# Graph kernel: dense adjacency built two pairs to a bank and emptied by two engines, one-hots by scalar comparison, type embeddings in one matmul, packed slices

## The chip, the cores and the metric

The kernel runs on one core of a Trainium2 chip. Times are device microseconds of one execution; three runs of the kernel before gave 7442.04, 7473.25 and 7475.92 us, a median of 7473.25.

## The reference

Two message-passing layers with residual and layer norm over a graph of 6250 nodes and 206,250 edges sorted by destination. The first is a two-layer mean aggregation. The second, which the change is about, has three relational convolutions with 5 edge types; the first of them takes a node's 128 features joined with the 128 of its type's embedding (3 types):

```python
def rgcn_conv(x, src, dst, etype, W, root, bias):
    seg = dst * R + etype                      # R = 5 relations
    agg = segment_sum(x[src], seg, n * R)
    cnt = segment_sum(ones, seg, n * R)
    agg = where(cnt > 0, agg / max(cnt, 1), 0).reshape(n, R, -1)
    return einsum('nrd,rdk->nk', agg, W) + x @ root + bias

h = concatenate([x, node_emb[node_type]], -1)
h = relu(rgcn_conv(h, ..., W1, root1, b1))     # 256 -> 256
h = relu(rgcn_conv(h, ..., W2, root2, b2))     # 256 -> 128
h = relu(rgcn_conv(h, ..., W3, root3, b3))     # 128 -> 128
```

## The kernel before, in words

The first 1480 us or so make the mean-aggregation layer, and as a by-product, codes of the edges. Then conv 1, 2 and 3 run (v = 0, 1, 2 in the code), each as its own loop over half ticks, written out on every engine; what stands in a half tick on an engine is run in that order, and semaphores join the engines.

**Groups.** A tick (two half ticks) handles one group of 4 tiles of 128 edges. GpSimd gathers the messages of the source nodes by four indirect DMAs (L1373), up to 6 groups ahead. VectorE makes a one-hot of where each edge's sum goes (L1628, 4 groups ahead), TensorE multiplies (12 matmuls at L1386, and in conv 1 four narrow ones at L1390 for the types), and VectorE adds the result to running sums (L1650, L1651). Conv 1 has 403 groups and covers all nodes so; conv 2 and 3 have 235 each, for 28 of 49 tiles of nodes.

**Windows.** Every 16 ticks or so the sums of 256 nodes are whole. In `finish`, VectorE scales them (L1690, for features and types), clears them (L1697) and makes node_hot, the one-hot of the nodes' types (L1726). TensorE then makes the products with W1 in fp32 (L1461 to L1464, both halves of the 256 outputs): per half and relation one with the features and one with the types, and the two of the root. After ScalarE's relu TensorE makes the rows of the next convolution's table (L1470, L1444), which ScalarE and VectorE split in three bf16 pieces (VectorE's part at L1707 and L1712, where it waits for ScalarE), and SP stores them.

**The dense adjacency.** For the last 21 tiles of nodes conv 2 and 3 use a dense matrix of edge counts in place of gathers. It is built within conv 1, beside the groups. In a tick VectorE makes the one-hots of 4 pairs of nodes (`dense_onehots`, L1637, two buffers), TensorE builds 4 pairs, one matmul of 490 columns each, into two banks by turns (`build`, L1401), and ScalarE copies each bank to `stage` as fp8 (`evict`, L1523): a pair's two columns go next to each other, at a step of 32 bytes. Every 16 pairs ScalarE issues three DMAs that store the stage (L1532). 336 ticks, from the third of conv 1 on, have such one-hots. In conv 2 and 3 SP loads the matrix in slices (L1246, three for a chunk and relation) and the table's rows in pieces, and TensorE multiplies (L1421), some 22 matmuls in a tick.

## Time and profile before

| | |
|---|---|
| runs | 7442.04, 7473.25, 7475.92 us |
| profiled execution, own time | 7472.03 us |
| its span | 7469.8 us |
| TensorE (PE) busy | 5533.5 us, 74% |
| weight loads (PEld) | 3186.3 us |
| VectorE (DVE) busy | 2387.7 us, 32% |
| ScalarE (ACT) busy | 2078.3 us, 28% |
| GpSimd (POOL) busy | 3856.8 us, 52% |
| mean granted clock of TensorE | 0.793 |

Busy time is from start to end of an instruction's work; instructions of one engine that overlap are counted once. The clock is a share of full speed. In a timeline, rows of an engine that follow each other with the same line and shape are merged, with their count behind an x, and the idle time before them stands in brackets with what ended it. A releaser "issue" is nothing that the profile shows, "remote" is one that it can't name. A matmul in fp32 leaves two records.

### The profile page before, as it was taken

What the parts mean: (1) busy time and instruction counts of PE and PEld (TensorE: products, weight loads), DVE (VectorE), ACT (ScalarE), POOL (GpSimd) and SP (SyncE); (2) the same over time, 40 slices, a digit from 0 to 9 for tenths busy, and PEclk for the clock granted to TensorE, in tenths of its full rate; (3) what the DMA queues carried; (4) which work ended last, traced back from release to release, by engine and by line L of the source; (5) the groups of instructions that cost most, each with busy time, mean ns of one, the idle gap of its engine ahead of it and who ended that gap; (6) DMA issues with size and microseconds to landing.
All of it is one profiled execution on the core that took longest, in us unless ns stands there. A gap on an engine that the chain in (4) does not pass through costs nothing.

```text
span 7469.8 us, 91271 instructions
## 1 busy us (share of the span) xinstructions
PE 5533.5 (74%) x35088; PEld 3186.3 (43%) x35088; DVE 2387.7 (32%) x5451; ACT 2078.3 (28%) x3054; POOL 3856.8 (52%) x3575
## 2 busy tenths in 40 slices
PE   2777799956677666777667546888888878888887
PEld 1454466523333333333333233444444544454444
DVE  6776641233333333433333211111111211111112
ACT  2444430046565655666555000000000000000000
POOL 4000000076666666767665553666666656666665
PEclk6888899956666666666666566999999989999999
DMA  2222226433333333333333223455455444444443
GB/s 72 118 85 101 97 103 239 185 98 109 91 103 95 109 87 98 102 101 98 101 95 101 67 83 110 140 168 167 137 169 163 140 150 142 145 143 137 138 143 108
DMA packets 689816, 903.43 MB, mean 121 GB/s; under 512 B 73166, under 2 KB 605444, under 8 KB 685412
## 3 DMA queue, kind: packets, MB, share of 16 engines
q1 hardware_dynamic: 335292, 453.57, 18.0%
q0 software_dynamic: 169216, 348.44, 16.8%
q10 hardware_dynamic: 184872, 95.53, 4.4%
q8 instruction: 282, 4.62, 0.2%
q14 instruction: 154, 1.26, 0.1%
HBM read 692.22 MB, written 205.05 MB: 120 GB/s over the span
## 4 chain that ended last, share of the span: by engine, by line
PE 44%; ACT 12%; issue 9%; another core or an unknown queue 8%; DVE 4%; ACTq 2%; DVEq 0%; DMA 0%; POOL 0%; POOLq 0%
PE bank L1421 21%; ACT stage L1523 12%; PE bank L1386 7%; PE bank L1461 4%; PE bank L1462 4%; PE bank L1401 3%; PE bank L1444 2%; ACTq L1532 2%; PE bank L1390 1%; DVE scaled L1690 1%; PE bank L1463 1%; PE bank L1464 1%; DVE type_scaled L1690 1%; PE bank L1470 1%
## 5 line engine op out<-in xcount | busy, mean ns | idle before, releaser
L1373 POOL DMA_INDIRECT messages<-table,src_rows x2552 | 2873.0, 1126 | 1582.2 <-issue 711.9
L1421 PE MATMUL bank<-slices,pieces 128*128 128x384 fp8e4 x10290 | 1983.5, 337 | 363.8 <-issue 351.1
L1523 ACT CAST stage<-bank 128x490 fp8e4<-128x490 f32 x1344 | 1458.5, 1270 | 1063.8 <-PE bank L1401 820.0
L1421 PEld LDWEIGHTS bank<-slices,pieces 128*128 128x128 bf16 x10290 | 988.5, 100 | 1206.1 <-issue 702.3
L1373 POOL DMA_INDIRECT messages<-table,rel_rows x940 | 900.0, 957 | 586.1 <-issue 251.4
L1401 PE MATMUL bank<-rel_hot,lo_dense_hot 128*128 128x490 bf16 x1344 | 647.2, 521 | 675.3 <-ACT stage L1523 506.7
L1386 PE MATMUL bank<-group_hot,messages 128*128 128x120 bf16 x10476 | 875.6, 245 | 238.4 <-issue 99.8
L1651 DVE TENSOR_TENSOR sums<-sums,bank 128x120 f32 x873 | 236.5, 271 | 2299.9 <-remote 1823.0
L1386 PEld LDWEIGHTS bank<-group_hot,messages 128*128 128x128 bf16 x10476 | 777.0, 113 | 395.5 <-issue 239.3
L1650 DVE TENSOR_TENSOR type_sums<-type_sums,bank 3x120 f32 x403 | 107.9, 268 | 1913.2 <-PE bank L1390 1280.6
L1355 POOL IOTA iota_rel_i<- 128x490 int32 x1 | 1.4, 1395 | 1355.8 <-DMA table<-typed_rows 1355.8
L1401 PEld LDWEIGHTS bank<-rel_hot,lo_dense_hot 128*128 128x128 bf16 x1344 | 120.4, 103 | 1107.7 <-ACT stage L1523 787.7
L966 ACT CAST adjacency<-bank 128x400 bf16<-128x400 f32 x784 | 391.9, 504 | 436.3 <-PE bank L844 431.7
L868 PE MATMUL bank<-adjacency,x_pieces 128*128 128x384 bf16 (+1 forms) x2499 | 485.6, 337 | 0.0
L844 PE MATMUL bank<-q_hot,lo_hot 128*128 128x100 bf16 x3136 | 232.1, 222 | 264.2 <-DVE rd_hot L1048 255.5
L1461 PE MATMUL bank<-scaled,w 128*128 128x256 f32 (+1 forms) x500 | 300.5, 705 | 149.2 <-issue 149.2
L1598 ACT ACTIVATE rstd<-moments,eps 128x2 f32<-128x2 f32 (+1 forms) x21 | 6.2, 296 | 1440.6 <-DVE moments L1779 1068.6
L868 PE MATMUL bank<-adjacency,h_pieces 128*128 128x384 bf16 (+1 forms) x2499 | 398.9, 320 | 0.0
L1637 DVE TENSOR_TENSOR rel_hot<-iota_rel,rel_dense 128x1960 bf16<-128x1960 f16 x336 | 389.8, 1160 | 0.0
L1578 ACT ACTIVATE h_wide<-h_wide 128x256 f32<-128x256 f32 (+1 forms) x21 | 9.5, 452 | 1231.0 <-issue 633.1
L1628 DVE TENSOR_TENSOR group_hot<-iota,group_code 128x480 bf16<-128x480 f16 x873 | 347.6, 399 | 1.6
L844 PEld LDWEIGHTS bank<-q_hot,lo_hot 128*128 128x128 bf16 x3136 | 194.2, 106 | 340.2 <-DVE rd_hot L1048 253.1
(249 smaller groups left out, 4344.6 us busy)
## 6 DMA issues: line engine op xcount, KB each, us to landing
slices<-relations_d SPq DMA_DIRECT2D x140, 768.0 KB
adjacency_d<-adjacency SPq DMA_DIRECT2D x15, 4704.0 KB, 14.5
adjacency<-adjacency_d SPq DMA_DIRECT2D x15, 4704.0 KB, 15.0
slices<-relations_d SPq DMA_DIRECT2D x70, 816.0 KB
relations_d<-stage ACTq DMA_DIRECT2D x168, 320.0 KB
messages<-table,src_rows POOLq DMA_INDIRECT x2552
inverse<-inverse_d SPq DMA_DIRECT2D x52, 640.0 KB
relations_d<-stage ACTq DMA_DIRECT2D x84, 340.0 KB
```

The lines of the kernel that those rows point to most:

```text
L844: mm = pe.matmul(to[:, m * PAIR_COLS:(m + 1) * PAIR_COLS], lo_hot[:, i % 2, pair, :], q_hot[:, i % 2, pair, :], start=True, stop=True)
L868: mm = pe.matmul(bank[SUM_BANKS[k % 2]][:, 0:cols], pieces[:, h, piece, :], adjacency[HALF[c]][:, h, 0:cols], start=(m == 0), stop=(m == N ...
L966: act.copy(to, pairs).then_inc(evicted, 1)
L1373: pool.indirect_dma_start(messages[:, i % MESSAGES, t, 0:ROWS[v]], None, GATHERED[v], bass.IndirectOffsetOnAxis(ap=rows[:, e:e + 1], axis= ...
L1386: mm = pe.matmul(to[:, 0:GROUP_COLS], messages[:, i % MESSAGES, t, piece * P:(piece + 1) * P], group_hot[:, i % MESSAGES, t, :], start=(t ...
L1401: pe.matmul(bank[REL_BANKS[p % 2]][:, 0:REL_COLS], lo_dense_hot[:, b % 2, m, :], rel_hot[:, b % 2, m, :], start=True, stop=True).then_inc( ...
L1421: mm = pe.matmul(bank[DENSE_BANKS[K % 2]][:, 0:CHUNK], pieces[M % PIECE_RING][:, tile % PIECE_TILES, piece * P:(piece + 1) * P], slices[:, ...
L1461: pe.matmul(to, w1[:, r, f_cols], scaled[:, r, 0:cols], start=(r == 0), stop=False)
L1462: pe.matmul(to, emb_1[:, r * WIDE + half * P:r * WIDE + (half + 1) * P], type_scaled[:, r, 0:cols], start=False, stop=False)
L1523: act.copy(stage[:, u % 2, :, 2 * m:2 * m + 2], bank[REL_BANKS[p % 2]][:, 0:REL_COLS].rearrange("p (c d) -> p c d", d=2), saturate=False). ...
L1628: vec.tensor_tensor(group_hot[:, i % MESSAGES, :, :].rearrange("p k (c t) -> p k c t", t=2), iota16[:, 0:GROUP_COLS].rearrange("p (c t) -> ...
L1637: op = vec.tensor_tensor(hot[:, b % 2, :, :].rearrange("p u (c t) -> p u c t", t=2), iota[:, 0:cols].rearrange("p (c t) -> p c t", t=2).un ...
```

## The change

1. *Builds.* Two pairs (a couple) are built at once, in two parts: part 0 has the columns of tiles 0 to 24 (250 a pair), part 1 those of tiles 25 to 48 (240 a pair). Each part has one bank of its own, that holds both pairs. ScalarE copies part 0 out, VectorE part 1, each pair's two bytes next to the other's, so four in a row. Each part has its own semaphore. The stage's store (two DMAs, ScalarE's queue) comes 3 half ticks after its last couple.
2. *One-hots of the builds.* In place of two comparisons of two tensors for 4 pairs there are eight of a tensor with one fp32 number per partition, two for each pair.
3. *Type embeddings.* The 5 products of types and the root's of a half become one, whose 18 rows are the 6 x 3 types; SP copies the scaled type sums and node_hot of each window to partitions 32 to 49 by six DMAs, and the embeddings once. TensorE waits for them behind the sixth product of the first half, and no longer for node_hot.
4. *Slices.* Two for a chunk and relation (25 and 24 tiles) instead of three, loaded without gaps; 3 of them in the ring instead of 4, and 8 pieces of the table instead of 9.

```diff
-SLICE_TILES = (17, 16, 16)
+SLICE_TILES = (25, 24)
-SLICE_RING = 4
+SLICE_RING = 3
-PIECE_RING = PIECE_BLOCKS + 2
+PIECE_RING = PIECE_BLOCKS + 1
...
+            sp.wait_ge(emb_kept, 1)
+            for r in range(RELATIONS + 1):
+                at = EMB_AT + r * NODE_TYPES
+                sp.dma_start(emb_1[at:at + NODE_TYPES, 0:WIDE], emb_1[0:NODE_TYPES, r * WIDE:(r + 1) * WIDE] if r < RELATIONS else emb_root[:, :]).then_inc(emb_in, 16)
             for w in range(WINDOWS_1):
                 first = w * WINDOW
+                sp.wait_ge(scaled_made, w + 1)
+                sp.wait_ge(nodes_spread, w + 1)
+                sp.wait_ge(window_psum, w)
+                for r in range(RELATIONS + 1):
+                    at, cols = EMB_AT + r * NODE_TYPES, window_cols(0, w)
+                    sp.dma_start(type_scaled[at:at + NODE_TYPES, 0, 0:cols], type_scaled[0:NODE_TYPES, r, 0:cols] if r < RELATIONS else node_hot[:, 0:cols]).then_inc(typed_in, 16)
...
-            def build(p):
-
-                b, m = divmod(p, BATCH)
+            def build(j):
+
+                b, m = divmod(2 * j, BATCH)
                 if m == 0:
                     pe.wait_ge(rel_hot_made, b + 1)
-                if p >= 2:
-                    pe.wait_ge(rel_evicted, p - 1)
-                pe.matmul(bank[REL_BANKS[p % 2]][:, 0:REL_COLS], lo_dense_hot[:, b % 2, m, :], rel_hot[:, b % 2, m, :], start=True, stop=True).then_inc(rel_psum, 1)
+                for n in range(SLICES):
+                    if j:
+                        pe.wait_ge(rel_evicted[n], j)
+                    of_part = slice(2 * SLICE_FIRST[n], 2 * (SLICE_FIRST[n] + SLICE_TILES[n]))
+                    width = 2 * SLICE_TILES[n] * RELATIONS
+                    for q in range(2):
+                        hot = rel_hot[:, b % 2, m + q, :].rearrange("p (r c) -> p r c", r=RELATIONS)[:, :, of_part]
+                        mm = pe.matmul(bank[REL_BANKS[n]][:, q * width:(q + 1) * width], lo_dense_hot[:, b % 2, m + q, :], hot, start=True, stop=True)
+                    mm.then_inc(rel_psum, 1)
...
-                        pe.wait_ge(nodes_spread, w + 1)
...
+                            if half:
+
+                                pe.wait_ge(typed_in, 16 * (RELATIONS + 1) * (w + 1))
+                                pe.matmul(to[0], emb_all[:, f_cols[0]], typed_all[:, 0:cols], start=False, stop=True)
                             for r in range(RELATIONS):
-                                pe.matmul(to, w1[:, r, f_cols], scaled[:, r, 0:cols], start=(r == 0), stop=False)
-                                pe.matmul(to, emb_1[:, r * WIDE + half * P:r * WIDE + (half + 1) * P], type_scaled[:, r, 0:cols], start=False, stop=False)
-                            pe.matmul(to, w1_root[:, f_cols], x1_T[:, nodes], start=False, stop=False)
-                            mm = pe.matmul(to, emb_root[:, f_cols], node_hot[:, 0:cols], start=False, stop=True)
-                        mm.then_inc(window_psum, 1)
+                                pe.matmul(to[half], w1[:, r, f_cols[half]], scaled[:, r, 0:cols], start=(r == 0), stop=False)
+                            pe.matmul(to[half], w1_root[:, f_cols[half]], x1_T[:, nodes], start=False, stop=False)
+                        pe.matmul(to[1], emb_all[:, f_cols[1]], typed_all[:, 0:cols], start=False, stop=True).then_inc(window_psum, 1)
...
+        def evict(engine, n, j):
+
+            u, m = divmod(j, STAGE_COUPLES)
+            engine.wait_ge(rel_psum, j * SLICES + n + 1)
...
+            from_bank = bank[REL_BANKS[n]][:, 0:4 * SLICE_TILES[n] * RELATIONS].rearrange("p (q c d) -> p c q d", q=2, d=2)
+            to = stage[:, u % 2, rows, 4 * m:4 * m + 4].rearrange("p c (q d) -> p c q d", q=2)
+            if n == 0:
+                engine.copy(to, from_bank, saturate=False).then_inc(rel_evicted[n], 1)
+            else:
+                engine.tensor_copy(to, from_bank, saturate=False).then_inc(rel_evicted[n], 1)
...
                 if b >= 2:
-                    vec.wait_ge(rel_psum, (b - 1) * BATCH)
-                for hot, codes, iota, cols in ((lo_dense_hot, lo_dense, iota16, P), (rel_hot, rel_dense, iota_rel, REL_COLS)):
-                    op = vec.tensor_tensor(hot[:, b % 2, :, :].rearrange("p u (c t) -> p u c t", t=2),
-                                           iota[:, 0:cols].rearrange("p (c t) -> p c t", t=2).unsqueeze(1).broadcast_to([P, BATCH, cols // 2, 2]),
-                                           codes[:, pairs, :].unsqueeze(2).broadcast_to([P, BATCH, cols // 2, 2]), ALU.is_equal)
+                    vec.wait_ge(rel_psum, (b - 1) * SLICES * BATCH // 2)
+                for m in range(BATCH):
+
+                    vec.tensor_scalar(lo_dense_hot[:, b % 2, m, :], iota16[:, :], lo_dense[:, b * BATCH + m:b * BATCH + m + 1], None, ALU.is_equal)
+                    op = vec.tensor_scalar(rel_hot[:, b % 2, m, :], iota_rel[:, :], rel_dense[:, b * BATCH + m:b * BATCH + m + 1], None, ALU.is_equal)
                 op.then_inc(rel_hot_made, 1)
...
+                    if v == 0 and 0 <= couple_at(half - 1) < COUPLES:
+                        evict(vec, 1, couple_at(half - 1))
```

VectorE, at the end of a window within conv 1, before the change (group_hot is the groups' one-hot, sums and type_sums the running sums, scaled and type_scaled the finished window):

```order
L1628 TENSOR_TENSOR group_hot<-iota_49,group_code 128x480 [waits group_psum]
L1644 TENSOR_LOAD base_i
L1650 ISA [waits sums_added,group_psum]
L1650 TENSOR_TENSOR type_sums<-type_sums,bank 3x120
L1651 REGISTER_ALU
L1651 TENSOR_TENSOR sums<-sums,bank 128x120
L1637 TENSOR_TENSOR lo_dense_hot<-iota_49,lo_dense 128x512 [waits rel_psum]
L1637 TENSOR_TENSOR rel_hot<-iota_rel,rel_dense 128x1960
L1690 TENSOR_TENSOR scaled<-sums,inverse 128x1280 [waits window_psum,inverse_in1,sums_added]
```

The same place on VectorE, with the change:

```order
L1690 ISA [waits sums_added,group_psum]
L1690 TENSOR_TENSOR type_sums<-type_sums,bank 3x120
L1691 REGISTER_ALU
L1691 TENSOR_TENSOR sums<-sums,bank 128x120
L1678 TENSOR_SCALAR lo_dense_hot<-iota_49,lo_dense 128x128 [waits rel_psum]
L1679 TENSOR_SCALAR rel_hot<-iota_rel,rel_dense 128x490
L1678 TENSOR_SCALAR lo_dense_hot<-iota_49,lo_dense 128x128
L1679 TENSOR_SCALAR rel_hot<-iota_rel,rel_dense 128x490
L1678 TENSOR_SCALAR lo_dense_hot<-iota_49,lo_dense 128x128
L1679 TENSOR_SCALAR rel_hot<-iota_rel,rel_dense 128x490
L1678 TENSOR_SCALAR lo_dense_hot<-iota_49,lo_dense 128x128
L1679 TENSOR_SCALAR rel_hot<-iota_rel,rel_dense 128x490
L1560 CAST stage<-bank 128x120x4 [waits rel_psum] x2
```

Two copies of part 1 (one at the end of each half tick) now stand between the one-hots and what followed them; both wait for a build. The first belongs to the couple that was built ahead of the group whose sums were just added.

TensorE in a tick of builds, before the change (group_hot and messages are the group's, rel_hot and lo_dense_hot the builds'):

```order
L1401 MATMUL bank<-rel_hot,lo_dense_hot 128x490 [waits rel_evicted] x3
L1386 MATMUL bank<-group_hot,messages 128x120 [waits gathered0,group_hot_made,sums_added]
L1386 MATMUL bank<-group_hot,messages 128x120 x11
L1390 MATMUL bank<-group_hot,messages 3x120 x4
L1401 MATMUL bank<-rel_hot,lo_dense_hot 128x490 [waits rel_evicted,rel_hot_made]
```

TensorE with the change, with the block of a window in fp32 (L1495, L1496; L1493 and L1497 are the type products) in front of the second couple of a tick, and the group behind it (L1408, L1412):

```order
L1495 MATMUL bank<-scaled,w_126 128x256 [waits wide_made,scaled_made]
L1495 MATMUL bank<-scaled,w_126 128x256 x4
L1496 MATMUL bank<-x_T,w_root 128x256
L1493 MATMUL bank<-type_scaled,emb_130 128x256 [waits typed_in]
L1428 MATMUL bank<-rel_hot,lo_dense_hot 128x250 [waits rel_evicted0]
L1428 MATMUL bank<-rel_hot,lo_dense_hot 128x250
L1428 MATMUL bank<-rel_hot,lo_dense_hot 128x240 [waits rel_evicted1]
L1428 MATMUL bank<-rel_hot,lo_dense_hot 128x240
L1408 MATMUL bank<-group_hot,messages 128x120 [waits gathered3,group_hot_made,sums_added]
L1408 MATMUL bank<-group_hot,messages 128x120 x11
L1412 MATMUL bank<-group_hot,messages 3x120 x4
L1428 MATMUL bank<-rel_hot,lo_dense_hot 128x250 [waits rel_evicted0,rel_hot_made]
```

Where a build waited for a copy two builds back, each part now waits for the copy of the same part one couple back.

## Rows read from the trace of the kernel before

**Rows 1.** Busy time by stretch: us, busy by engine, granted clock, DMA share, GB/s
```profile
1521.00:4076.00 2555.00, 1801.79 (x8034) 890.35 (x8034) 953.34 (x1929) 1503.07 (x1512) 1694.97 (x1346) 0.63 0.34 98
4140.00:4560.00 420.00, 225.36 (x1129) 133.14 (x1126) 92.76 (x222) 17.06 (x36) 199.36 (x198) 0.59 0.23 66
```

**Rows 2.** The chain of waits in 1521 to 4076 us, by line
```profile
by line: ACT stage L1523 34.1%; PE bank L1461 9.1%; PE bank L1462 9.0%; issue 7.8%; PE bank L1401 7.5%; PE bank L1386 6.3%; ACTq L1532 4.7%; PE bank L1444 4.6%; another core or an unknown queue 4.3%; PE bank L1390 2.7%; PE bank L1463 1.8%; 
```

**Rows 3.** By tile or line: count, ns min/median/max, first and last start
```profile
L1637 DVE TENSOR_TENSOR rel_hot<-iota_rel,rel_dense x336: 1158/1160/1173, 1521.6 to 4075.8; 128x1960 bf16<-128x1960 f16 x168
...
L1461 PE MATMUL bank<-scaled,w x500: 421/634/797, 1641.2 to 4570.4; 128*128 128x256 f32 x160, 128*128 128x128 f32 x7
```

**Rows 4.** Timeline, ticks with builds: start us, us, engine, line, operation
```profile
2989.79 0.79 PE L1386 MATMUL bank<-group_hot,messages 128*128 128x120 bf16 x12
2990.51 0.37 PE L1390 MATMUL bank<-group_hot,messages 128*3 128x120 bf16 x4
...
2996.31 1.40 PE L1386 MATMUL bank<-group_hot,messages 128*128 128x120 bf16 x12
...
3001.06 0.59 PE L1401 MATMUL bank<-rel_hot,lo_dense_hot 128*128 128x490 bf16 x1 [0.44 <-ACT stage L1523]
...
3001.44 1.41 PE L1386 MATMUL bank<-group_hot,messages 128*128 128x120 bf16 x12
...
3002.78 0.56 PE L1390 MATMUL bank<-group_hot,messages 128*3 128x120 bf16 x4
3002.92 0.95 POOL L1373 DMA_INDIRECT messages<-table,src_rows  x1 [0.30 <-issue]
...
3003.47 0.27 DVE L1650 TENSOR_TENSOR type_sums<-type_sums,bank 3x120 f32 x1 [2.93 <-issue]
...
3003.86 0.41 DVE L1637 TENSOR_TENSOR lo_dense_hot<-iota,lo_dense 128x512 bf16<-128x512 f16 x1
3003.89 4.32 ACT L1523 CAST stage<-bank 128x490 fp8e4<-128x490 f32 x4 [0.82 <-PE bank L1401]
3004.18 2.33 POOL L1373 DMA_INDIRECT messages<-table,src_rows  x1 [0.30 <-issue]
3004.19 1.16 DVE L1637 TENSOR_TENSOR rel_hot<-iota_rel,rel_dense 128x1960 bf16<-128x1960 f16 x1
...
3005.28 0.39 DVE L1628 TENSOR_TENSOR group_hot<-iota,group_code 128x480 bf16<-128x480 f16 x1
...
3017.96 1.41 PE L1386 MATMUL bank<-group_hot,messages 128*128 128x120 bf16 x12
```

**Rows 5.** Timeline around the block of one window
```profile
3031.63 2.48 DVE L1690 TENSOR_TENSOR scaled<-sums,inverse 128x1280 f32<-128x1280 f32 x1
...
3032.96 1.41 PE L1386 MATMUL bank<-group_hot,messages 128*128 128x120 bf16 x12
...
3039.29 0.34 DVE L1726 TENSOR_SCALAR node_hot<-types_in,j_col 3x256 f32<-3x256 int32 x1
...
3039.73 1.19 PE L1461 MATMUL bank<-scaled,w 128*128 128x256 f32 x2 [3.95 <-issue]
...
3068.09 1.41 PE L1386 MATMUL bank<-group_hot,messages 128*128 128x120 bf16 x12
```

**Rows 6.** VectorE's groups by shape (count, busy, mean ns), and one stretch of its timeline
```profile
L1088 DVE TENSOR_TENSOR mean<-bank,inv_deg 128x384 f32<-128x384 f32 x32 | 17.8, 556 | 342.9 <-PE bank L868 180.5 <-DMA residual_d<-mean 162.4
L584 DVE TENSOR_SCALAR passed<-j,last_f 128x3136 bf16<-128x3136 f16 x13 | 12.4, 1031 | 0.0
L1088 DVE TENSOR_TENSOR mean<-bank,inv_deg 128x128 f32<-128x128 f32 x2 | 0.6, 292 | 9.8 <-DMA x_rows<-residual_d 5.9 <-PE bank L868 4.0
...
9.09 12.39 DVE L584 TENSOR_SCALAR passed<-j,last_f 128x3136 bf16<-128x3136 f16 x13
```

**Rows 7.** The page's costliest groups: count, busy us, mean ns, idle before
```profile
L1421 PE MATMUL bank<-slices,pieces 128*128 128x384 fp8e4 x10290 | 1983.5, 337 | 363.8 <-issue 351.1
...
L966 ACT CAST adjacency<-bank 128x400 bf16<-128x400 f32 x784 | 391.9, 504 | 436.3 <-PE bank L844 431.7
```

More of the change, by code:

```diff
@@ L476, in keep_span @@
                     turned_codes = bank[CODE_BANKS[n]][:, 0:width // 2].bitcast(f16)
+                    if n == 0 and s >= FIRST_DENSE_SPAN:
+                        first = max(0, FIRST_DENSE_PAIR - s * SPAN)
+                        act.copy(lo_plain[:, SPAN_PAIRS[s]], turned_codes[:, first:width])
                     act.copy(to[:, cols, :], turned_codes.unsqueeze(2).broadcast_to([P, width, 2])).then_inc(span_kept, 1)
@@ L485, in keep_rel @@
                 turned_codes = bank[CODE_BANKS[0]][:, first // 2:(first + width) // 2].bitcast(f16)
[L486 removed]
+                act.copy(rel_code[:, cols], turned_codes).then_inc(rel_kept, 1)
             keep_span(0)
@@ L1506, in conv_tensor @@
                     if v == 0:
-                        first = (half - 2 * (REL_TICK + 1)) * (BATCH // 2)
-                        for p in range(max(0, first), min(first + BATCH // 2, DENSE_PAIRS)):
-                            build(p)
+                        if 0 <= couple_at(half) < COUPLES:
+                            build(couple_at(half))
                     if v == 2 and half - 2 in plan.task_end:
```

91 lines of the change are left out of this document (49 added, 42 removed).

## The prediction

> **What bounds the kernel now.** I read the stretches first, then the chain of waits, then one tick in the timeline. The change touches the first relational convolution, in which ticks with dense builds run from 1521.6 to 4075.8 us: 336 of them, one per pair of one-hot instructions [rows 3], 7.6 us each. In that stretch no engine is full: TensorE is busy 1802 of 2555 us at a granted clock of 0.63, ScalarE 1503, VectorE 953, GpSimd 1695 [rows 1]. The chain says who is waited for: ScalarE's copies out of the banks (stage L1523) are 34% of it, the two families of wide fp32 matmuls L1461 and L1462 9% each [rows 2].
>
> The timeline shows how. Two ScalarE copies stand between the builds and two beside the group's 16 matmuls; four take 4.32 us, 1.07 each [rows 4], and every fourth tick also issues three DMAs on ScalarE. Four ticks from 2996.31 to 3017.96 take 21.65 us, 5.4 each [rows 4]. The end of a window puts in one block of 24 fp32 products: from one group at 3032.96 to the next at 3068.09 are 35.1 us, of which the block from 3039.73 is about 27.6, so 1.15 us a product (the profile has two records for one) [rows 5]. It waited for node_hot, made at 3039.29 + 0.34 [rows 5]. Blocks start from 1641.2 to 4570.4, 500 records at 20 a block, so 25 blocks [rows 3]: about 20 beside the builds (every 122 us until 4075.8), 4 full ones behind them, and a last one of half width. The 316 build ticks without a block share 2554 - 20 x 35.1 = 1852 us.
>
> GpSimd is near but not the bound: a gather takes 0.95 us and 0.30 between two, yet one that starts within VectorE's run of one-hots takes 2.33 [rows 4]. With one such gather a tick that is 4 x 1.25 + 1.38 = 6.4 us a tick at worst; in the stretch it is busy 1695 of 2555 us.
>
> **The change, part by part.** *Where the new wait sits.* A bank now holds two pairs of one part of the columns, so a build needs its own bank emptied, with no second bank to alternate with. Part 0 is emptied by ScalarE, part 1 by VectorE. VectorE's copy for the second couple of a tick stands behind the next group's adds and behind the eight new one-hot instructions, and TensorE's second part of the following build waits for it, in front of everything else on TensorE. So a loop through both engines closes twice a tick. At TensorE's lower clock, from one VectorE copy's end to its like a tick later:
> - TensorE starts after 0.10 (3039.63 to 3039.73 [rows 5]); 480 columns at the pace of 490 in 0.38 (3001.06 to 3001.44); the group from 3001.44 to 3002.78 + 0.56, 1.90; VectorE starts at 3003.47, 0.13 later; its two adds until 3003.86, 0.39 [rows 4]: 2.90.
> - Eight TENSOR_SCALARs. Thirteen of 3136 f16 elements take 12.39 us, the last lasting 1.03, so 0.947 from start to start [rows 6]. On VectorE a column from PSUM costs (556 - 292) / 256 = 1.03 ns [rows 6]; at a quarter of that 3136 cost 0.81, and 0.14 stay per instruction. So 490 columns 0.27, 128 columns 0.17, and four of each 1.7 us, against 3003.86 to 3005.28 = 1.42 for the two instructions of now [rows 4].
> - VectorE's copy, 480 columns of fp32 from PSUM: 292 ns at 128 columns plus 352 x 1.03 = 0.65.
> - Release 0.10, the part's 480 columns with their latency 0.52, release 0.13, the second copy 0.65: 1.40.
>
> Together 6.65 us. At the high clock (a group from 2989.79 to 2990.51 + 0.37 is 1.09 instead of 1.90, and 0.2 less on each part) it is 5.45. The granted 0.63 of [rows 1] is 26% of the time at 2.4 GHz and the rest at 1.2, so 6.34 on average. ScalarE, with two copies and fewer DMAs a tick, falls off the path; what it did cost ends, and the tick of 5.4 becomes 6.34. The runs of stores and the ticks with table matmuls gain and lose a little each; I take +1.0 us for each of 316 ticks: **+316**.
>
> The copy's price is not in the trace: ScalarE's of the same kind costs 1.07 for 490, while its fp32-to-bf16 copy of 400 takes 0.50 [rows 7]. From below it is 0.57 (0.07 fixed, as between the two one-hots that start at 3003.86 and 3004.19, 512 columns in 0.33 at 0.26 + 0.07), from above ScalarE's 1.06. I take 0.65, the rows of VectorE itself.
>
> The Trainium skill (SBUF — State Buffer, under "Door 1: The DMA port swizzle") says that two accesses in one 16-byte line suffice for full rate. The copy of now writes two bytes at a step of 32 and takes 1.07 us, so this trace does not agree; by the rule the new copy with four bytes in a row would be 0.65, and if ScalarE's rate holds per element, 1.06.
>
> *The type embeddings.* Twelve of the 24 products are of type embeddings; two take their place, so 14 stay: 10 x 1.15 = 11.5 us less. Beside builds the gain is smaller: VectorE goes through scale, memsets and node_hot from 3031.63 to 3039.56 (7.9 us) [rows 5], and only then through 0.33 group one-hots, 0.39 adds, 1.7 and 0.65 to the copy that TensorE needs in front of the block. So from the group's start the block begins after 10.6 + 0.5 instead of 6.8, takes 16.1, and two builds follow: 28.0 instead of 35.1, or **-144** for 20. Behind the builds this doesn't hold; there the block also need not wait for node_hot (3.2 us), but its seventh product waits for six small copies by DMA, issued one after the other on SP behind node_hot (I take 1.7 us of a possible -3 to +5): -13 for each of 4, -7 for the last: **-59**.
>
> *Row pieces.* VectorE's four subtractions per window now stand in the loop; half of each is hidden by the part's matmuls: **+12** for 20 windows.
>
> *Packed slices, ring of 3, ring of pieces 8.* The loads become one run a partition. TensorE waited for nothing named there: 1.98 ms of dense matmuls with 351 us of "issue" before them [rows 7]. I cost it at nothing; it is bounded by those 351 us on one side and, if the shorter ring of pieces is late at four changes of relation, by 4 x 10 us on the other. Earlier stages: a few copies of 0.6 us, nothing.
>
> Sum on the profiled execution, 7472.0 us (median of the three 7473.25): +316 - 144 - 59 + 12 = +125, so **7597 us**.
>
> The Trainium skill (VectorE: DVE Perf Modes, "Rules for kernel authors") advises few VectorE instructions rather than fused ones, since each pays a fixed cost. [rows 6] agree with 0.14 us each; it speaks against eight one-hots in place of two, which the fourfold rate (same page, "The perf-mode tier table") would otherwise favour. By element rate alone they would take 0.6 us, by the rule 1.7.
>
> **Rivals.** *VectorE's pieces are cheap (faster).* If only 0.07 is fixed per instruction, one-hots take 1.2 and a copy 0.57, the loop 5.99 and 5.68 on average: +0.34 x 316 + 12 - 156 (each block starts 0.6 sooner) - 59 = -96, 7376 us. For it: the spacing of the two one-hots of now. Against: two kinds of rows with 0.14 or more [rows 6]. It decides from a loop of 5.9 us down, where the block's gain wins.
> *The fp8 copy costs on VectorE what it costs on ScalarE.* 1.06 instead of 0.65 twice: +0.82 x 316 + 8, 7864 us. For it: the same destination, steps of 32 bytes. Against: twice as many bytes in a row, another engine.
> *The clock.* If TensorE is granted 2.4 GHz half of the time, the loop is 6.05 and the sum +32, 7505 us. Behind the builds, with TensorE busy 225 of 420 us, it was 0.59 [rows 1], so a looser load doesn't promise it.
> *The slices.* If a third of the 351 us came from their many small packets: 7480 us. Nothing in the rows ties them.
> *ScalarE's relief shows and no loop forms.* It would need VectorE's copy in front of its one-hots; the order shows it behind.
>
> **How the numbers follow.** Forecast 0.50 (7520 to 7690); dear copy 0.16; cheap pieces 0.17; clock 0.09 and slices 0.08, mostly within 0.5%, which is 7436 to 7511 and about what a measurement tells from no change. So faster 0.20, same 0.12, slower 0.68. The range of 7430 to 7870 leaves out the cheap end and what lies above the dear copy.
>
> **What would show it.** In the profile after: groups of four ticks 25 us apart instead of 21.65; TensorE's second part released by VectorE and not ScalarE; ScalarE busy under half of the stretch; eight TENSOR_SCALARs in 1.7 us; a VectorE copy of 0.65; blocks of 16 us and 28 from group to group; later convolutions of equal length. I am wrong if the first part's release by ScalarE still ends the waits, if the tick stays under 5.9 us, or if the gain lies behind 4600 us.

## The result, and the profile after

The changed kernel takes 7379.94 us (median of 4 runs, 7372.54 to 7387.85) against 7461.24 of the kernel before (4 runs): ratio 0.9883, 95% interval 0.9862 to 0.9904. That is 1.2% faster, where 7597 us and 1.7% slower were forecast; it lies 50 us below the lower end of the range. Its profiled execution took 7384.1 us, span 7382.3.

Of the 87.5 us between the two spans, this is where they come and go. A "tick" is the time from one group to the next; there are 336 with builds, 20 of them with a block of fp32 products in them. The builds are counted from VectorE's first one-hots to its last.

| us | before | after | difference | forecast |
|---|---|---|---|---|
| start of the builds | 1521.6 | 1531.8 | +10 | 0 |
| 316 build ticks without a block | 1852 (5.86 each) | 2122 (6.715 each) | +270 | +328 |
| 20 ticks over a block | 702 (35.1 each) | 401 (20.05 each) | -301 | -144 |
| last one-hots to the last block | 494.6 | 427.3 | -67 | -59 |
| last block to the end | 2899.4 | 2900.2 | +1 | 0 |

(+328 is +316 and the +12 for the row pieces.) The stretch with builds and the one behind them, columns as in [rows 1]:

```profile
1532.00:4055.00 2523.00, 1450.11 (x8970) 918.27 (x8970) 1442.00 (x4609) 455.12 (x845) 1439.71 (x1342) 0.64 0.35 99
4140.00:4470.00 330.00, 149.13 (x1012) 109.24 (x1011) 80.89 (x208) 17.07 (x36) 181.00 (x184) 0.65 0.29 82
```

ScalarE's busy time fell from 1503 to 455 us, VectorE's rose from 953 to 1442, and TensorE's is 352 us less at nearly the same mean clock. The chain of waits in 1532 to 4055 us, which answers to [rows 2]:

```profile
by line: PE bank L1428 14.6%; PE bank L1408 13.2%; DVE rel_hot L1679 13.1%; DVE stage L1560 12.2%; DVE lo_dense_hot L1678 8.7%; issue 7.2%; PE bank L1412 5.7%; PE bank L1495 5.1%; PE bank L1473 4.9%; DVE sums L1691 3.4%; DVE scaled L1730 1.
```

ScalarE's copy, 34% before, is gone from it, and VectorE's one-hots (L1678, L1679) and copy (L1560) are 34% together. The products of a block are 5.1% on the new line L1495, where L1461 and L1462 had 18. First and last start by tile and line, as in [rows 3]:

```profile
L1679 DVE TENSOR_SCALAR rel_hot<-iota_rel,rel_dense x1344: 330/332/522, 1531.8 to 4054.8; 128x490 bf16<-128x490 f16 x192
...
L1495 PE MATMUL bank<-scaled,w x500: 379/622/796, 1661.9 to 4482.1; 128*128 128x256 f32 x160, 128*128 128x128 f32 x7
```

One plain tick in the timeline, at the place of [rows 4]:

```profile
3000.45 1.41 PE L1408 MATMUL bank<-group_hot,messages 128*128 128x120 bf16 x12
3001.78 0.56 PE L1412 MATMUL bank<-group_hot,messages 128*3 128x120 bf16 x4
...
3002.68 0.26 DVE L1691 TENSOR_TENSOR sums<-sums,bank 128x120 f32 x1
3002.87 0.23 DVE L1678 TENSOR_SCALAR lo_dense_hot<-iota,lo_dense 128x128 bf16<-128x128 f16 x1
...
3004.55 0.64 DVE L1560 CAST stage<-bank 128x480 fp8e4<-128x480 f32 x1
3005.24 0.53 PEld L1428 LDWEIGHTS bank<-rel_hot,lo_dense_hot 128*128 128x128 bf16 x4 [2.84 <-DVE stage L1560]
...
3005.86 0.66 DVE L1560 CAST stage<-bank 128x480 fp8e4<-128x480 f32 x1 [0.68 <-PE bank L1428]
...
3006.95 1.41 PE L1408 MATMUL bank<-group_hot,messages 128*128 128x120 bf16 x12
```

The circle, the loop of waits through TensorE and VectorE, stands as the prediction drew it: group, adds, eight one-hots in 1.68 us (3002.87 to 3004.55), copy 0.65, second part of the next build, copy 0.65, group. It takes 6.50 us at the lower clock (6.65 forecast). The block, at the place of [rows 5]:

```profile
3037.01 4.48 PE L1495 MATMUL bank<-scaled,w 128*128 128x256 f32 x10
...
3041.29 1.06 PE L1496 MATMUL bank<-x_T,w_root 128*128 128x256 f32 x2
...
3042.28 0.87 PE L1493 MATMUL bank<-type_scaled,emb 18*128 18x256 f32 x2
3043.08 2.43 PE L1495 MATMUL bank<-scaled,w 128*128 128x256 f32 x10
...
3045.34 0.59 PE L1496 MATMUL bank<-x_T,w_root 128*128 128x256 f32 x2
...
3046.49 0.60 PE L1428 MATMUL bank<-rel_hot,lo_dense_hot 128*128 128x250 bf16 x4
```

It is over in 9.5 us (3037.01 to 3046.49), not in 16.1; the 20 blocks beside builds last 8.9 in the mean, 8.2 to 9.6. Its first five wide products take 4.28 us, 0.86 each, and the five of the second half 2.26, 0.45 each. The clock of the same time (us, TensorE busy, granted clock as a share of 2.4 GHz, DMA share, GB/s):

```profile
3037.00:3040.00 3.00, 3.00 (x9) 0.50 0.17 41
3040.00:3043.00 3.00, 3.00 (x8) 0.55 0.00 0
3043.00:3046.50 3.50, 3.50 (x16) 1.00 0.00 0
3046.50:3058.00 11.50, 6.94 (x59) 1.00 0.43 128
```

and of the block before the change, 48 records without a gap:

```profile
3040.00:3067.00 27.00, 27.00 (x48) 0.50 0.16 42
```

So both halves of the block's gain have to be explained: what it costs per product, and that TensorE comes up to 2.4 GHz in it and stays there for a while behind it.

### The profile page after: what moved, and what is told of

Same layout as the page of the kernel before. It is cut to its first block, busy times and chain, and to the rows that moved or that the text cites. A ratio compares the mean times of both kernels' runs of the same rounds, so it can differ in the third digit from the quotient of the medians.

```text
span 7382.3 us, 95103 instructions
## 1 busy us (share of the span) xinstructions
PE 5100.1 (69%) x35932; PEld 3189.8 (43%) x35932; DVE 2881.2 (39%) x8139; ACT 1023.3 (14%) x2385; POOL 3605.2 (49%) x3575
## 4 chain that ended last, share of the span: by engine, by line
PE 44%; DVE 18%; issue 8%; another core or an unknown queue 7%; DVEq 1%; DMA 1%; SPq 0%; ACT 0%; POOL 0%; POOLq 0%
PE bank L1450 22%; PE bank L1408 9%; PE bank L1428 5%; DVE rel_hot L1679 4%; DVE stage L1560 4%; DVE lo_dense_hot L1678 3%; PE bank L1412 2%; PE bank L1495 2%; PE bank L1473 2%; DVE sums L1691 1%; DVE scaled L1730 1%; DVE type_scaled L1730 1%; DVE sums L1737 1%; PE bank L1521 0%
## 5 line engine op out<-in xcount | busy, mean ns | idle before, releaser
L1395 POOL DMA_INDIRECT messages<-table,src_rows x2552 | 2621.1, 1027 | 1773.1 <-PE bank L1412 802.7
L1428 PE MATMUL bank<-rel_hot,lo_dense_hot 128*128 128x240 bf16 (+1 forms) x2688 | 651.6, 362 | 1093.3 <-DVE stage L1560 1013.5
L1408 PE MATMUL bank<-group_hot,messages 128*128 128x120 bf16 x10476 | 911.3, 252 | 251.3 <-issue 132.9
L1408 PEld LDWEIGHTS bank<-group_hot,messages 128*128 128x128 bf16 x10476 | 817.7, 118 | 379.4 <-issue 227.4
L1428 PEld LDWEIGHTS bank<-rel_hot,lo_dense_hot 128*128 128x128 bf16 x2688 | 213.7, 111 | 1449.2 <-DVE stage L1560 1227.9
L1558 ACT CAST stage<-bank 128x500 fp8e4<-128x500 f32 x672 | 387.1, 576 | 2117.6 <-PE bank L1428 1992.0
L1560 DVE CAST stage<-bank 128x480 fp8e4<-128x480 f32 x672 | 434.1, 646 | 184.6 <-PE bank L1428 182.2
L1679 DVE TENSOR_SCALAR rel_hot<-iota_rel,rel_dense 128x490 bf16<-128x490 f16 x1344 | 450.5, 335 | 0.0
L1678 DVE TENSOR_SCALAR lo_dense_hot<-iota,lo_dense 128x128 bf16<-128x128 f16 x1344 | 336.3, 250 | 0.3
L877 PEld LDWEIGHTS bank<-adjacency,h_pieces 128*128 128x128 bf16 x2499 | 238.4, 98 | 151.8 <-issue 3.8
```

Of the source, the lines that this page charges most:

```text
L877: mm = pe.matmul(bank[SUM_BANKS[k % 2]][:, 0:cols], pieces[:, h, piece, :], adjacency[HALF[c]][:, h, 0:cols], start=(m == 0), stop=(m == N ...
L1395: pool.indirect_dma_start(messages[:, i % MESSAGES, t, 0:ROWS[v]], None, GATHERED[v], bass.IndirectOffsetOnAxis(ap=rows[:, e:e + 1], axis= ...
L1408: mm = pe.matmul(to[:, 0:GROUP_COLS], messages[:, i % MESSAGES, t, piece * P:(piece + 1) * P], group_hot[:, i % MESSAGES, t, :], start=(t ...
L1428: mm = pe.matmul(bank[REL_BANKS[n]][:, q * width:(q + 1) * width], lo_dense_hot[:, b % 2, m + q, :], hot, start=True, stop=True)
L1558: engine.copy(to, from_bank, saturate=False).then_inc(rel_evicted[n], 1)
L1560: engine.tensor_copy(to, from_bank, saturate=False).then_inc(rel_evicted[n], 1)
```

## Experiments

Theory A: the products of 3 rows, in turn with those of 128, are what keeps TensorE at 1.2 GHz in the block, and each costs more than its columns. Rival B: the looser loop ahead of the block lets the clock rise. Rival C: the gain is the number of products.

Runs of one letter ran on one chip, each letter on a chip of its own. On that of the f runs the kernel before took 7462 us, as in the result; on the other three 6853 to 6857. Each ratio is against the kernel before on the same chip. The table puts their profiles side by side (builds here from TensorE's first to its last; "block" is the mean of 20 from group to group over a block, "tick" what is left of the builds for each of the other 316; "to last block" and "to end" follow one another).

| kernel | us | ratio [95%] | block | tick | builds | to last block | to end |
|---|---|---|---|---|---|---|---|
| c0 before | 6860 | | 35.3 | 5.71 | 2512 | 387 | 2456 |
| c1 changed | 6840 | 0.997 [0.996, 0.998] | 20.0 | 6.74 | 2531 | 347 | 2454 |
| e1 changed, old block | 7298 | 1.065 [1.063, 1.067] | 39.7 | 6.82 | 2949 | 386 | 2456 |
| e2 before, new block | 6497 | 0.948 [0.947, 0.950] | 18.7 | 5.76 | 2192 | 347 | 2450 |
| e3 narrow ones grouped | 6589 | 0.961 [0.960, 0.963] | 22.9 | 5.70 | 2260 | 355 | 2453 |
| e4 24 of 128 rows | 6509 | 0.949 [0.948, 0.951] | 19.3 | 5.73 | 2198 | 350 | 2454 |
| d1 24 of 3 rows | 6702 | 0.977 [0.975, 0.978] | 28.7 | 5.73 | 2384 | 361 | 2458 |
| d2 64 and 128 in turn | 6855 | 0.999 [0.999, 1.000] | 35.5 | 5.70 | 2510 | 385 | 2455 |
| f1 24 of 64 rows | 7296 | 0.977 [0.974, 0.979] | 28.5 | 5.84 | 2417 | 452 | 2896 |
| f2 64 rows grouped | 7110 | 0.951 [0.948, 0.954] | 19.9 | 5.96 | 2282 | 411 | 2893 |
| d3 packed slices alone | 6806 | 0.992 [0.991, 0.994] | 35.5 | 5.54 | 2461 | 387 | 2460 |
| c2 copy first | 6288 | 0.918 [0.916, 0.919] | 18.0 | 5.13 | 1980 | 348 | 2456 |
| c3 both copies by ScalarE | 6226 | 0.909 [0.907, 0.910] | 19.5 | 4.83 | 1916 | 359 | 2449 |
| d4 c3, type rows sooner | 6217 | 0.907 [0.905, 0.908] | 14.0 | 5.12 | 1897 | 359 | 2456 |

**e1, the changed kernel with the old block.**

```diff
...
-                        pe.matmul(to[1], emb_all[:, f_cols[1]], typed_all[:, 0:cols], start=False, stop=True).then_inc(window_psum, 1)
...
+                            for r in range(RELATIONS):
+                                pe.matmul(to, w1[:, r, f_cols], scaled[:, r, 0:cols], start=(r == 0), stop=False)
+                                pe.matmul(to, emb_1[:, r * WIDE + half * P:r * WIDE + (half + 1) * P], type_scaled[:, r, 0:cols], start=False, stop=False)
...
```

> The changed kernel with the type embeddings of the first convolution put back as they were: 24 products a block, every second one of 3 rows, no copies by SyncE. Theory A (the 3-row products keep TensorE's granted clock at 0.50): the block goes back to about 27 us and from group to group over it 35 us, so 20 blocks x 15 us and the 67 us behind the builds come back: 7380 + 301 + 67 = about 7748 us. Rival B (TensorE idles longer ahead of a block in the new loop, and that, not the products, let the clock rise): the block shows a clock above 0.7 with the 24 products too and takes about 20 us, 7600 us or less.

The block is back at 39.7 us, and inside it TensorE is busy without a gap at a clock of 0.50:

```profile
2362.00:2390.00 28.00, 28.00 (x55) 0.50 0.00 1
```

Rival B falls: the new loop does not raise the clock by itself. The time of 7748 us was not met because this chip is faster elsewhere; against the changed kernel (c1, on another chip of the same pace) it is +458 us, where +368 was expected: the old block costs 4.3 us more from group to group in the new loop than in the old, though it lasts as long by itself (27.5 and 27.6 us).

**e2, the kernel before with the new block alone.** The twelve narrow products become two of 18 rows, with SyncE's copies of the rows; nothing else changes.

```diff
...
-                                pe.matmul(to, emb_1[:, r * WIDE + half * P:r * WIDE + (half + 1) * P], type_scaled[:, r, 0:cols], start=False, stop=False)
...
+                        pe.matmul(to[1], emb_all[:, f_cols[1]], typed_all[:, 0:cols], start=False, stop=True).then_inc(window_psum, 1)
```

> The kernel before with only the type embeddings changed (one product of 18 rows a half in place of six of 3, the rows gathered by SyncE). Theory A (narrow products hold the clock): the block takes about 9.5 us here as well, 20 x -15 us in the loop and -60 behind it: 7461 - 301 - 60 = 7100 us. Rival B (the lighter loop of the changed kernel gave the clock back): the 14 products stay at a clock of 0.50 and 16 us, 20 x -7 - 59 = 7460 - 200 = 7260 us. Rival C (the gain came from the builds): 7400 us or more.

356 us come off: 20 x 16.6 in the blocks and 40 behind the builds, less 16 in the other ticks. But the block itself is not the 9.5 us of Theory A. It lasts 15.0 in the mean, because TensorE waits 3.4 to 5.8 us behind the sixth product for SyncE's copies; in each of the 20 blocks the clock falls back to 0.50 in this wait or within 2 us behind it:

```profile
2370.00 0.59 PE L1481 MATMUL bank<-x_T,w_root 128*128 128x256 f32 x2
2376.26 1.22 PE L1478 MATMUL bank<-type_scaled,emb 18*128 18x256 f32 x2 [5.67 <-DMA type_scaled<-node_hot]
```

In the changed kernel the block starts later in the tick, when the copies are there, and has no such wait beside builds. So this one part of the change, with its wait, is worth 5.2%; all of it together is worth 0.3% on such a chip (c1), so the rest of the change costs nearly what this part earns.

**e3, the same 24 products in another order.**

```diff
                             for r in range(RELATIONS):
                                 pe.matmul(to, w1[:, r, f_cols], scaled[:, r, 0:cols], start=(r == 0), stop=False)
-                                pe.matmul(to, emb_1[:, r * WIDE + half * P:r * WIDE + (half + 1) * P], type_scaled[:, r, 0:cols], start=False, stop=False)
                             pe.matmul(to, w1_root[:, f_cols], x1_T[:, nodes], start=False, stop=False)
+                            for r in range(RELATIONS):
+                                pe.matmul(to, emb_1[:, r * WIDE + half * P:r * WIDE + (half + 1) * P], type_scaled[:, r, 0:cols], start=False, stop=False)
```

> The kernel before with the same 24 products a block in another order: in each half the six of 128 rows first, then the six of 3 rows. Theory A1 (a narrow product costs or holds the clock wherever it stands): the first half's wide products start at 1.2 GHz, the narrow ones hold it there, block 24 to 27 us, time 7400 to 7461 us. Theory A2 (the alternation does it: weights of 3 and of 128 rows in turn): block 9.5 us for the wide ones and 3 to 5 us for the narrow ones, about 14 us, -12 x 21 = 7200 us.

Nothing is taken away, and 264 us come off. The clock in one block, by runs of products (128 rows, 3 rows, 128 rows, 3 rows):

```profile
2388.40:2393.80 5.40, 5.33 (x12) 0.50 0.22 59
2393.80:2396.60 2.80, 2.80 (x13) 0.98 0.39 95
2396.60:2401.10 4.50, 4.50 (x13) 0.62 0.28 72
2401.10:2404.00 2.90, 2.90 (x14) 1.00 0.36 93
```

It rises at the end of a run of 128 rows, falls back behind the run of 3 rows, and rises again. The narrow products then run at 0.45 us each. The block lasts 15.3 us in the mean, nearer to A2's 14 than to A1's 24 to 27, and -264 us is near A2's -252.

**e4, 24 products of 128 rows.**

```diff
-                                pe.matmul(to, emb_1[:, r * WIDE + half * P:r * WIDE + (half + 1) * P], type_scaled[:, r, 0:cols], start=False, stop=False)
+                                pe.matmul(to, w1[:, r, f_cols], scaled[:, r, 0:cols], start=False, stop=False)
...
-                            mm = pe.matmul(to, emb_root[:, f_cols], node_hot[:, 0:cols], start=False, stop=True)
+                            mm = pe.matmul(to, w1_root[:, f_cols], x1_T[:, nodes], start=False, stop=True)
```

> The kernel before with 24 products a block, all of 128 rows: each narrow product is replaced by a repeat of the wide one beside it, so the type embeddings are left out and the rest is counted twice. Theory A (width, not number): the clock rises inside the block as in the changed kernel, 5 products x 0.86 + 19 x 0.41 = 12 us against 27.0, -15 x 20 - 60: about 7110 us although no product is taken away. Rival D (the number of products is what the block costs): 24 products stay at 1.15 us each, 7461 us or more.

Rival C (D in the text above) falls: as many products as before, more arithmetic, and the time of e2 within 12 us. (That the two are so near doesn't price the ten products more: e2 has its wait instead. The block lasts 12.6 us here and 8.9 in the changed kernel.) The block at work, and two of its products at the higher clock, 0.43 apart:

```profile
2373.00:2375.70 2.70, 2.70 (x7) 0.50 0.14 39
2375.70:2383.70 8.00, 8.00 (x38) 0.99 0.35 86
...
2376.67 0.59 PE L1461 MATMUL bank<-scaled,w 128*128 128x256 f32 x2
2377.10 0.59 PE L1462 MATMUL bank<-scaled,w 128*128 128x256 f32 x2
```

**c0 and c1, both kernels again on a chip of the faster kind.**

> The kernel before, unchanged, for its profile on the chip of this call. On the chip of the last call it took 6853 us against 7461 beside the changed kernel, and its conv 2 and 3 ended 2450 us after the last block in the three kernels derived from it, against 2900 us. Theory: the difference sits behind the builds, where the trace of the first chip has gaps of TensorE that it puts down to issue (351 us at the dense products), and these gaps are gone here; the block is 35 us or a little more, as in the first trace.

> The changed kernel, unchanged, on the chip of this call. Worked out from the run with the old block there (7298 us, 39.3 us over a block, last block at 4840): 20 x (39.3 - 20.1) = 385 and about 65 behind the builds come off, 6850 us: 1.00 of the kernel before. If the two parts add up in another way (Rival: the copies by SyncE cost more where the rest is faster), 6950 us or more.

Both expectations hold: 2456 us from the last block to the end against 2899, and the group of L1421, with 351 us of "issue" before it in [rows 7], has none:

```profile
L1421 PE MATMUL bank<-slices,pieces 128*128 128x384 fp8e4 x10290 | 1789.6, 330 | 0.0
```

The changed kernel is 0.3% faster here, not 1.2%. In the kernel before ScalarE bounds the loop, and on the chip of the result its copies also waited 146 us for issue and 89 for an unknown queue in 1525 to 3900 us, against 79 and nothing here; the changed kernel's ticks (6.715 and 6.74) are the same on both. Why the chips differ was not tried.

**c2, VectorE's copy at the head of the tick.**

```diff
                 for half in range(plan.end):
+                    if v == 0 and 0 <= couple_at(half - 1) < COUPLES:
+                        evict(vec, 1, couple_at(half - 1))
                     if half % 2 == 0 and half < plan.half_ticks:
```

(and taken out behind the one-hots.)

> The changed kernel with VectorE's copy of the even half put at the head of the tick, ahead of the one-hots and of the addition. Theory (the tick is a circle: addition 0.45, one-hots 1.68, copy 0.65, build, group 1.9): one of the two copies leaves the circle, the plain tick goes from 6.47 to 5.6-5.8 us, 316 x -0.8 = -250 us against the changed kernel. Rival (TensorE's own work at 1.2 GHz sets the tick): 6.3 us or more, -50 at most.

-552 us against c1, twice what was expected. Most of it is the circle. Two groups at 1.2 GHz now start 5.25 us apart, where the changed kernel needs 6.50:

```profile
2754.76 1.40 PE L1408 MATMUL bank<-group_hot,messages 128*128 128x120 bf16 x12
2760.01 1.41 PE L1408 MATMUL bank<-group_hot,messages 128*128 128x120 bf16 x12
```

With the one copy the part of a build and the two releases between the copies leave the circle too, the last 1.40 us of the prediction's list, and 6.65 - 1.40 is 5.25. That is about 316 x 1.25 = 395 us, an estimate; 40 more are in the blocks (18.0 for 20.0). The rest, some 117 us, goes with the clock. The busy time and clock of TensorE in 1600 to 3300 us, of c1 and of c2:

```profile
1600.00:3300.00 1700.00, 982.43 (x6047) 0.64 0.35 100
```

```profile
1600.00:3300.00 1700.00, 1109.68 (x7755) 0.74 0.45 128
```

In the tighter loop TensorE's mean clock is 0.74 instead of 0.64, and a group of twelve matmuls that takes 1.41 us at 1.2 GHz takes 0.79 at 2.4, so the circle gets shorter again. No run separates this share.

**c3, both parts copied by ScalarE.**

```diff
                             evict(act, 0, j)
+                            evict(act, 1, j)
...
-                    if v == 0 and 0 <= couple_at(half - 1) < COUPLES:
-                        evict(vec, 1, couple_at(half - 1))
```

> The changed kernel with both parts of a bank couple copied by ScalarE (0.576 us measured for 500 columns), none by VectorE. Theory (VectorE's order holds the bank): ScalarE needs 4 x 0.6 = 2.4 us of a tick, the banks come free at once, and the tick falls to what four gathers on GpSimd take, 4 x 1.3 = 5.2 us: 316 x -1.25 = -400 us against the changed kernel. Rival (ScalarE's copy becomes the bound again as in the kernel before, 1.07 us each): 4 x 1.1 = 4.4 us and the tick stays at 5.9 or more, -180 us at most.

-614 us against c1, more than expected, and by another way than the tick of 5.2. The copies cost ScalarE no more than VectorE:

```profile
L1558 ACT CAST stage<-bank 128x500 fp8e4<-128x500 f32 x1344 | 699.2, 574 | 1173.1 <-PE bank L1428 1161.9 <-issue 4.7 <-DMA relations_d<-stage 1.4
```

The new bound is GpSimd, which waits only 4 us for another engine. Its busy time in 1600 to 3300 us, and its waits there:

```profile
1600.00:3300.00 1700.00, 1336.23 (x1195) 0.75 0.46 132
```

```profile
POOL messages L1395 <- issue: 360.1, 1182, 0.3
POOL messages L1395 <- PE bank L1412: 4.0, 13, 0.3
```

1336 and 360 make 1696 of 1700 us, 1.42 for each of 1195 gathers. 336 ticks of four are 1908 us, and the builds take 1916.

**d1, 24 products of 3 rows.**

```diff
-                                pe.matmul(to, w1[:, r, f_cols], scaled[:, r, 0:cols], start=(r == 0), stop=False)
+                                pe.matmul(to, emb_1[:, r * WIDE + half * P:r * WIDE + (half + 1) * P], type_scaled[:, r, 0:cols], start=(r == 0), stop=False)
...
```

> The kernel before with 24 products a block of 3 rows each, the wide ones replaced by repeats of the narrow ones (the terms of the neighbours and of the node itself are left out of the first convolution's output). Theory N (products of 3 rows leave the granted clock at 0.50 however long TensorE is busy with them): the block shows 0.50 throughout and takes as long as before, 27 us and 35 us from group to group; 6857 us, ratio 0.99 to 1.00. Rival X (only the turn from 3 rows to 128 and back holds the clock): it rises as with 24 wide ones, block 12 to 15 us, -15 x 20 us: 6510 us, ratio 0.95.

**d2, 64 rows in turn with 128.**

```diff
-                                pe.matmul(to, emb_1[:, r * WIDE + half * P:r * WIDE + (half + 1) * P], type_scaled[:, r, 0:cols], start=False, stop=False)
+                                pe.matmul(to, w1[0:64, r, f_cols], scaled[0:64, r, 0:cols], start=False, stop=False)
...
```

> The kernel before with each narrow product replaced by one of 64 rows (the upper half of the wide one beside it, so the type embeddings are left out and half of the other rows are counted twice). If the height of the short products decides, this lies between the block of 24 wide ones (19.3 us from group to group, 6509 us) and the one of before (35.3 us, 6857 us). Theory N with 64 rows as good as 128: 6510 us; Rival X (any turn between two heights): 6857 us.

Theory N holds for the clock in d1 (0.50 throughout) and not for the time: 153 us come off. In d2 the time of before comes back to 1 us, with none of its narrow products. One block of d1, and one of d2, each with two of its products:

```profile
2205.30:2226.10 20.80, 20.76 (x49) 0.50 0.31 77
...
2206.32 1.06 PE L1462 MATMUL bank<-type_scaled,emb 3*128 3x256 f32 x2
2207.18 1.06 PE L1461 MATMUL bank<-type_scaled,emb 3*128 3x256 f32 x2
```

```profile
2238.80:2266.50 27.70, 27.68 (x49) 0.50 0.22 55
...
2239.94 1.22 PE L1462 MATMUL bank<-scaled,w 64*128 64x256 f32 x2
2241.09 1.22 PE L1461 MATMUL bank<-scaled,w 128*128 128x256 f32 x2
```

(The height of a product is the number of its rows; a turn is the change from one height to another.) At the same clock 24 products take 20.8 us without a turn and 27.7 with one at each: they start 0.853 apart in d1 (the mean) and 1.15 in d2, so a turn costs 0.30 us at 1.2 GHz, for 64 rows as for 3.

**f1 and f2, 64 rows without a turn, and with one turn a half.** f2 has d2's products in e3's order; f1 is d2 with the wide products cut to 64 rows as well:

```diff
-                                pe.matmul(to, w1[:, r, f_cols], scaled[:, r, 0:cols], start=(r == 0), stop=False)
+                                pe.matmul(to, w1[0:64, r, f_cols], scaled[0:64, r, 0:cols], start=(r == 0), stop=False)
...
```

> The kernel before with all 24 products of a block of 64 rows (the upper halves of the wide ones, each twice; the lower halves and the type embeddings are left out). Theory H (the height decides: what is below 128 rows leaves the clock at 0.50): 0.50 throughout as with 24 of 3 rows, 28.7 us from group to group, 6700 us. Theory T (the turn from one height to another decides): the clock rises as with 24 of 128 rows, 19.3 us, 6510 us.

> The kernel before with 12 products of 128 and 12 of 64 rows a block, the six of 128 first in each half and the six of 64 behind them (the same products as in the run with 64 rows in turn, 6855 us, 35.5 us from group to group). Theory H: the clock falls again in the runs of 64 rows, as with 3 rows grouped, about 23 us and 6590 us. Theory T: one turn a half does nothing, 19.5 us and 6515 us. If neither, 6855 us: the mean height of the block decides, in whatever order.

f1 is d1 again (ratio 0.977 both), at 0.50 for the whole block, as Theory H has it. f2 is nearly e4 (0.951 and 0.949), as Theory T has it: here the clock does not fall in the runs of 64 rows. One block of f1; then one of f2 by runs:

```profile
2242.90:2263.70 20.80, 20.79 (x49) 0.50 0.27 68
```

```profile
2204.20:2209.30 5.10, 5.06 (x13) 0.54 0.26 64
2209.30:2212.00 2.70, 2.70 (x13) 1.00 0.31 74
2212.00:2214.80 2.80, 2.80 (x13) 1.00 0.40 94
2214.80:2217.70 2.90, 2.90 (x14) 1.00 0.30 80
```

So neither height nor turn alone is the answer. In the 20 blocks of each of these runs the clock rose only in a run of 128-row products or up to 0.8 us behind its end; 64 rows did not raise it (f1) but kept it (f2), in or just behind a run of 3 rows it fell (e3), and with 64 or 3 rows in turn with 128 it did not rise in a single block (d2, c0, e1, before). Which one quantity the chip goes by is open.

**d3, packed slices alone** (with the view of a slice to match).

```diff
-SLICE_TILES = (17, 16, 16)
+SLICE_TILES = (25, 24)
-SLICE_RING = 4
+SLICE_RING = 3
-PIECE_RING = PIECE_BLOCKS + 2
+PIECE_RING = PIECE_BLOCKS + 1
```

> The kernel before with only the slices packed (25 and 24 tiles in place of 17, 16 and 16, rings of 3 and 8). Theory (TensorE is the bound of the dense products and the packets are hidden): within 0.3% of before, ratio 1.000; from the last block to the end 2450 us as before. Rival (fewer packets feed the slices sooner, or the shorter ring of pieces starves): 20 us or more either way behind the last block.

The dense products are unchanged to 4 us, but 50 us (0.8%) come off in the builds. The one part of d3 that runs beside the builds is the stores: three a stage on ScalarE become two. Its timeline in before and here:

```profile
2991.62 1.95 ACTq L1532 DMA_DIRECT2D relations_d<-stage  x3
```

```profile
2382.70 1.22 ACTq L1533 DMA_DIRECT2D relations_d<-stage  x2
```

84 stages of four ticks at 0.6 to 0.7 us are 50 to 60 us, while ScalarE bounds the loop. The expectation had looked only behind the last block.

**d4, c3 with the copies of the type rows let go sooner.**

```diff
-                sp.wait_ge(nodes_spread, w + 1)
                 sp.wait_ge(window_psum, w)
                 for r in range(RELATIONS + 1):
+                    if r == RELATIONS:
+                        sp.wait_ge(nodes_spread, w + 1)
```

> The changed kernel with both copies by ScalarE as in the last call (6226 us there), and SyncE's first five copies of the type rows let go as soon as they are scaled: only the sixth waits for the one-hots of the nodes. In the last trace TensorE waits 4.5 us in a block for the sixth. Theory: five issues (3.4 us) come out of that wait, 3 us x 21 blocks = -60 us: 6165 us, ratio 0.899. Rival (the clock that TensorE lost in the wait comes back later only, or the wait moves to the second half): 6210 us or more.

The block falls from 19.5 to 14.0 us, more than expected, but the time by 9 and not by 60, with intervals of the ratios that overlap. Of the 110 us saved in the blocks 92 come back in the other ticks (5.12 for 4.83), because GpSimd sets the pace through both. c3 and d4 are the best versions found, 9% under either kernel.

## Why the prediction was wrong

**The step that failed is the block**: "14 stay: 10 x 1.15 = 11.5 us less", "takes 16.1", 28.0 from group to group, -144. It took 9.5, and 20.05; -301. The 1.15 us of [rows 5] held two costs that left with the narrow products, the turn and the lower clock. At 1.2 GHz a product takes 0.853 (d1) and a turn to another height 0.30 (d2); at 2.4 GHz a product takes 0.43 (e4). Fourteen products at 1.15 are 16.1; measured are seven in 6.07 us and seven in 3.41 (from 3037.01 to 3043.08 and on to 3046.49). The count, the only thing that the prediction priced, was worth least. By the mean length of a block: 27.6 us before, 20.8 without turns (d1), 12.6 with the clock that rises (e4), 8.9 with 14 products instead of 24 (changed). So 6.8 us went with the turns, 8.2 with the clock and 3.7 with the count, for which 11.5 were forecast.

The prediction never asked for the clock inside the block, and so took over its 1.2 GHz with the price. The trace before showed that something held it there: TensorE was busy without a gap for 27 us and still at 0.50, while in [rows 4] a group of the loop ran at 0.79 us. The Trainium skill (TensorE: Matmul & The Clock Gate, "What's actually happening") ties the clock to how busy the engine has been, and by that rule the block should have run at 2.4 GHz already; this trace does not agree (27.65 us busy of 27.70 at 0.50 in c0), and nor do d1, d2 and f1. The Trainium skill (TensorEngine Tiling (Array Packing), "Key Properties") says that a change of tiling mode drains the engine; the 0.30 us between d2 and d1 agrees, if a height of 64 or less is another mode, which no run shows.

**The loop was right in its mechanism and a little too dear.** +0.855 us a tick against +1.0: plain ticks 6.50 (6.65), one-hots 1.68 (1.7), VectorE's copy 0.646 (0.65). The 274 ticks with neither a block nor table matmuls grew by 0.99 (5.46 to 6.45 in the mean), as forecast; the mis-sized part is the 40 ticks with the table's matmuls, which grew by 0.25 (8.6 to 8.9) and not by 1.0. By the rule of the Trainium skill (SBUF — State Buffer, "Door 1: The DMA port swizzle") a copy with two accesses in a line has the full rate. For VectorE's copy the rows gave 0.65 at full rate, and the trace agrees; it does not for the copy of before, which took 1.07 with two bytes in a row. c2 and c3 show that the circle, not the work, costs: with less of it the tick falls to 5.13, and without it to 4.83.

Two sums inside the -144 don't come out either: the terms in front of a block (7.9 + 0.33 + 0.39 + 1.7 + 0.65) end 9.7 us behind the group's start and not 10.6, and 20 x (28.0 - 35.1) is -142. The block shown starts 11.0 us behind its group (3025.99 to 3037.01), where 11.1 was forecast, so the start was right.

**Behind the builds** -67 against -59 is right by luck: two errors cancel. A block there lasts 15.3 to 16.0 us, since its products cost less than 1.15 each but TensorE waits 3.3 to 3.8 us for SyncE's copies, where 1.7 was taken:

```profile
4252.31 1.22 PE L1493 MATMUL bank<-type_scaled,emb 18*128 18x256 f32 x2 [3.83 <-DMA type_scaled<-node_hot]
```

**The convolutions after** +1 against 0. **The packed slices** at nothing were wrong as a part by itself (-50 us, d3, all of it beside the builds); that they give nothing in the changed kernel, where ScalarE has slack, is argued, not shown.

**The rivals.** "VectorE's pieces are cheap" gave nearly the time measured, 7376, by a mechanism that did not happen (one-hots 1.68 and not 1.2, copy 0.646 and not 0.57); that its number fits is luck. The clock was a rival too, but with its gain in the loop at large and for one chance in eleven. The clause "I am wrong if the tick stays under 5.9 us" did not come in; the error lay in a term that no clause watched.

## What to carry to other kernels

Ask of a duration read from a trace which of its parts would leave with the instruction beside it: here some 0.7 of a product's 1.15 us was its neighbour's doing. Keep matmuls of one height together, and pile small ones into one; in this kernel the order alone was worth 3.9% and the piling 5.2%. When an instruction that frees a bank goes to another engine, put it at the head of that engine's tick, not behind its own new work: here that alone turned 0.3% into 8.2%. And where small DMAs feed a block, see whether they land before it starts: in e2 TensorE waited 3.4 to 5.8 us for them.

## What the runs showed of the hardware that was not expected

- TensorE at 1.2 GHz though busy 27.65 of 27.70 us, with products of 128 rows in turn with 3 or 64 (before, d2), and busy 20.8 of 20.8 with 64 or 3 rows alone (f1, d1).
- 0.30 us more from start to start when the height of an fp32 product of 256 columns changes (1.15 and 0.853 at 1.2 GHz).
- ScalarE's copy from fp32 in PSUM to fp8: 500 columns with four bytes in a row at a step of 32 in 0.574 us, where 490 with two bytes in a row cost 1.07 from start to start [rows 4].
- Chips differ: the same work behind the last block took 2456 us on three chips and 2896 on that of the f runs (2899 in the result), and the dense matmuls had 351 us of "issue" before them in the profile before and none in c0.
